# Separate places for ScalarE's and VectorE's look-up steps, from two tables over the work list

## The reference

```python
def _ghost_linear(x, idx, lut):
    w = lut[idx]                                  # weights are looked up: idx is 0..15
    return jnp.einsum('bsh,oh->bso', x, w)

# attention, on the layer-normed x (2, 2048, 512):
q, k, v = x @ Wq, x @ Wk, x @ Wv
attn_scores = jnp.einsum('bes,bfs->bef', qT, kT) / np.sqrt(16)   # 512 x 512 for each batch
attn_weights = softmax(attn_scores); out = (attn_weights @ vT).T @ Wo

# ffn, on the layer-normed x: INTER = 1376, HIDDEN = 512
h = silu(_ghost_linear(x, gate_idx, lut)) * _ghost_linear(x, up_idx, lut)
return _ghost_linear(h, down_idx, lut)

x = x + attn(layernorm(x));  x = x + ffn(layernorm(x))
```

## Time and profile before

| | before |
|---|---|
| median of 3 runs | 1107.08 us (1107.05 to 1108.62) |
| the profiled execution | 1108.86 us, span 1107.0 us |
| busy over the span | PE 1028.1 us (93%), PEld 844.5 (76%), DVE 491.6 (44%), ACT 467.8 (42%), POOL 137.8 (12%) |
| mean granted TensorE clock | 0.973 of full speed |

### The profile page before, as it was taken

The page is one execution under the profiler, slowest core; times in us unless marked ns, Lnnn a source line. Parts: engine busy times, 40 slices in busy tenths (PEclk is TensorE's granted clock), DMA queues, the critical chain, the costliest instruction groups (busy, mean ns, idle before and its releaser), DMA issues.

```text
span 1107.0 us, 13011 instructions
## 1 busy us (share of the span) xinstructions
PE 1028.1 (93%) x4744; PEld 844.5 (76%) x4744; DVE 491.6 (44%) x1016; ACT 467.8 (42%) x753; POOL 137.8 (12%) x135
## 2 busy tenths in 40 slices
PE   5888986979889897999999999999999999999997
PEld 4777775767668775788888888888888888888885
DVE  5786867978878987332213122312221222212001
ACT  4987767777867884122122212211221222122110
POOL 4422000000000000002011111111111111111111
PEclk9988998989979999999999999999999999999999
DMA  8853010230101114530022000201020010000000
GB/s 280 266 198 91 8 60 6 84 119 6 46 8 65 60 51 158 207 129 1 1 76 77 1 1 1 78 1 62 15 76 1 1 41 36 1 1 38 1 1 38
DMA packets 31756, 66.04 MB, mean 60 GB/s; under 512 B 3584, under 2 KB 17168, under 8 KB 27088
## 3 DMA queue, kind: packets, MB, share of 16 engines
q1 hardware_dynamic: 26912, 63.06, 15.9%
q10 hardware_dynamic: 4752, 2.16, 0.7%
q0 software_dynamic: 32, 0.01, 0.1%
HBM read 44.18 MB, written 21.04 MB: 59 GB/s over the span
## 4 chain that ended last, share of the span: by engine, by line
PE 66%; DVE 12%; ACT 12%; issue 8%; POOL 1%; DMA 1%; ACTq 0%; POOLq 0%; DVEq 0%
PE bank L1050 34%; PE bank L1058 19%; PE bank L992 8%; ACT part L791 4%; DVE part L1237 3%; PE bank L1093 2%; DVE picked L1237 2%; ACT picked L791 1%; PE bank L1006 1%; PE bank L1039 1%; DVE bn L1214 1%; DVE w_lo L1253 1%; ACT idx_out L872 1%; DVE part L1275 1%; ACT xg_n L882 1%
## 5 line engine op out<-in xcount | busy, mean ns | idle before, releaser
L1050 PE MATMUL bank<-x2t_hi,w_hi 128*128 128x512 f32 (+1 forms) x704 | 278.3, 395 | 22.6 <-ACT h_gate L944 10.3
L1050 PE MATMUL bank<-x2t_hi,w_lo 128*128 128x512 f32 (+1 forms) x704 | 276.8, 393 | 0.0
L1050 PE MATMUL bank<-x2t_lo,w_hi 128*128 128x512 f32 (+1 forms) x704 | 276.6, 393 | 0.0
L1450 DVE TENSOR_TENSOR h_full<-bank,h_gate 128x512 f32<-128x512 f32 (+1 forms) x66 | 45.6, 691 | 396.6 <-PE bank L1050 396.6
L1050 PEld LDWEIGHTS bank<-x2t_hi,w_hi 128*128 128x128 f32 (+1 forms) x704 | 132.1, 188 | 55.6 <-issue 20.6
L791 ACT ACTIVATE part<-high_bit,lut,lut_step 128x512 f32<-128x512 uint8 x198 | 155.4, 809 | 27.3 <-DVE part L1237 24.9
L1050 PEld LDWEIGHTS bank<-x2t_lo,w_hi 128*128 128x128 f32 (+1 forms) x704 | 132.1, 188 | 30.3
L1050 PEld LDWEIGHTS bank<-x2t_hi,w_lo 128*128 128x128 f32 (+1 forms) x704 | 132.4, 188 | 29.5
L740 POOL TENSOR_TENSOR h_lo<-h_full,h_hi 128x512 fp32r<-128x512 f32 (+1 forms) x66 | 85.2, 1291 | 508.1 <-ACT h_hi L968 508.1
L965 ACT ACTIVATE h_gate<-bank 128x512 f32<-128x512 f32 (+1 forms) x66 | 39.4, 598 | 256.3 <-PE bank L1050 256.3
L1058 PE MATMUL bank<-w_hi,h_hi 128*128 128x512 f32 (+1 forms) x324 | 129.6, 400 | 0.1
(11 more groups left out here) (148 smaller groups left out, 1353.3 us busy)
## 6 DMA issues: line engine op xcount, KB each, us to landing
xg<-in_L_attn_x SPq DMA_DIRECT2D x8, 1024.0 KB, 6.3
out_dram<-x1a SPq DMA_DIRECT2D x5, 1024.0 KB, 3.9
x1a<-in_L_attn_x SPq DMA_DIRECT2D x4, 1024.0 KB, 4.8
x1b<-in_L_attn_x SPq DMA_DIRECT2D x3, 1024.0 KB, 4.8
m_hi<-m_scratch SPq DMA_DIRECT2D x3, 1024.0 KB, 5.1
m_lo<-m_scratch SPq DMA_DIRECT2D x3, 1024.0 KB, 7.2
out_dram<-x1b SPq DMA_DIRECT2D x3, 1024.0 KB, 3.9
idx_raw<-in_L_ffn_gate_idx SPq DMA_DIRECT2D x10, 256.0 KB, 6.2
```

Of the source, the lines that this page charges most:

```text
L1050: last = pe.matmul(tile[0:n, :], a, x, start=(k == 0 and j == 0), stop=(k == K - 1 and j == 2))
L1450: dve.tensor_tensor(h_full[0:n, :], bank[5][0:n, :], h_gate[0:n, :], ALU.mult).then_inc(h_done, 1)
```

## The change

The entries `look` and `built` leave the list, and with them `OPS`, `share`, `room` and the leaf tables. Each engine's look-up becomes a generator of single instructions (ScalarE: a leaf, a fetch, a copy to `w_hi`, 294 steps; VectorE: a find, a merge, a leaf, a `w_lo`, 429 steps). Two strings, `ACT_LOOKS` and `DVE_LOOKS`, have one digit (base 36) for each entry of the list: how many steps that engine takes ahead of that entry. The order of the look-up instructions among themselves is the same on both engines, and so are the other entries and their order, the waits, tiles and banks. Only which other instruction each step stands in front of is different, and no longer the same for both engines.

```diff
-        LEAVES_NEXT = {4: [1], 5: [0], 6: [3], 7: [2], 8: [5]}
-        LEAVES_SAME = {1: [6], 2: [7]}
...
-        def normalised(n, limit):
-            timeline.append(("norm", n))
-            look(1 if n < K * (number[(SCORE, 0)] + 1) else 2, limit)
-            timeline.append(("norm_low", n))
...
+        def normalised(n):
+            timeline.extend([("norm", n), ("norm_low", n)])
...
-            look(1, room(n))
             timeline.append(("take_low", n))
...
-        def share(cost):
-
-            passed[0] += cost
-            look(early + late * min(passed[0], whole) // whole - looked[0] if passed[0] < whole else OPS * U - looked[0], U)
...
+        ACT_LOOKS = (
+            "0000000000000000000000000000000000000000000000000000000000000000000000000000000000000001000000000000"
+            "1000000000101000000000000000000000030000000000000000000000000000000004000300000000000000000000000000"
+            "0000000300000000000000000000000000000000300000000000000000300000000010020200000000000500301020040030"
+            "0400300300500020000020000040000020000200002000040002000000000000000000000000000000600030000300400300"
+            "0030030000200500002002000200005000000010103000000003040000300000600205000020000007000100030500000000"
+            "020000060400060400304001050005050010500204000504003040020500040600106001080003050020400103"
+        )
+        DVE_LOOKS = (
+            "0000000000000000000000000000000000000000000000000000000000000000000000000000000000000000020000000001"
+            "0000000000000000000000010000000300000000000000000400000000000000000005000000030000000000000000000000"
+            "0000200000000000000200000000000000000010000000000003000000300000030000100000070000000030070005006004"
+            "0040050040026000030000040000060000030000300000006000040300000000000000000000000000070003000040060030"
+            "00045000000430000006200000420003000070011000600000003010200100900000a0200000008030006010007010000000"
+            "00200000d02000d020070200702000d010060100803000c010080200604000d020050400902000c050040300b"
+        )
+
+        def with_looks(counts, steps):
+            for k, entry in enumerate(timeline):
+                for _ in range(int(counts[k], 36) if k < len(counts) else 0):
+                    next(steps)
+                yield entry
...
+            def look_up():
+
+                yield from make_leaves(0, LEAVES[:LEAVES_AHEAD])
+                for u in range(U):
+                    yield from make_leaves(u, LEAVES[LEAVES_AHEAD:])
+                    if u + 1 < U:
+                        yield from make_leaves(u + 1, LEAVES[:LEAVES_AHEAD])
+                    act.wait_ge(picked_done, u + 1)
+                    if u + 3 < U:
+                        fetch_idx(u + 3)
+                        yield
+                    weight_high(u)
+                    yield
...
-            for stage, arg in timeline:
+            for stage, arg in with_looks(ACT_LOOKS, look_up()):
```

More of the change, by code:

```diff
@@ L280, in tile_of @@
             return picked[u % 2] if j == 0 else part[{1: one, 2: 1, 3: 2, 4: 3, 5: five, 6: one, 7: 2}[j]]
[L282 to L289, removed]
         def make_leaf(eng, u, j):
@@ L305, in preln_attention_ghost_ffn @@
         timeline = []
[L306 to L313, removed]
         def settle(g):
@@ L430, in preln_attention_ghost_ffn, with prepare @@
         second_plan = ("E10 E0 T0 E1 A0 T1 E2 A1 T2 E3 A2 T3 E4 A3 E5 E6 E7 X0 X1 E8 X2 X3 E9").split()
[L431 to L435, removed]
-        pair_order, second_down_order = [], []
-        passed = [0]
-        def share(cost):
-            passed[0] += cost
-            look(early + late * min(passed[0], whole) // whole - looked[0] if passed[0] < whole else OPS * U - looked[0], U)
-        def prepare(b, kind, i, looks):
+        pair_order, second_down_order = [], []
+        def prepare(b, kind, i):
             if kind == "T":
-                timeline.append(("turn", (b, i)))
-                looks()
-                timeline.extend([("turn_high", (b, i)), ("turn_low", (b, i))])
+                timeline.extend([("turn", (b, i)), ("turn_high", (b, i)), ("turn_low", (b, i))])
             elif kind == "A":
-                timeline.append(("attend", (b, i)))
-                looks()
-                timeline.append(("add", (b, i)))
+                timeline.extend([("attend", (b, i)), ("add", (b, i))])
                 if i == T - 1:
@@ L455, in prepare @@
             elif kind == "X":
-                timeline.append(("x2", (b, i)))
-                looks()
-                timeline.extend([("x2_high", (b, i)), ("x2_low", (b, i))])
+                timeline.extend([("x2", (b, i)), ("x2_high", (b, i)), ("x2_low", (b, i))])
         for step in first_plan:
             kind, i = step[0], int(step[1:])
-            cost = free_ns[kind]
             if kind in "GH":
@@ L465, in preln_attention_ghost_ffn @@
                 pair_order.append(item)
-                timeline.append(("gate_up", item))
-                share(cost // 2)
-                timeline.append(("silu", item))
+                timeline += [("gate_up", item), ("silu", item)]
                 if len(pair_order) == 1:
                     timeline.append(("ln1", 1))
-                share(cost - cost // 2)
                 timeline += [("h_full", item), ("h_high", item), ("h_low", item)]
@@ L474, in preln_attention_ghost_ffn @@
                 timeline.append(("down", (0, i)))
-                share(cost)
             else:
-                prepare(1, kind, i, lambda: share(cost))
-        assert looked[0] == OPS * U
+                prepare(1, kind, i)
         timeline += [("y", 0), ("stats1", 2), ("ln1", 2)]
@@ L784, in fetch_idx, with make_leaves @@
                 act.dma_start(idx_in[u % 3][:], idx_dram[u]).then_inc(idx_back[u % 3], 16)
-            def make_leaves(k):
-                if k == 0:
+            def make_leaves(u, some):
+                if u == 0:
                     act.wait_ge(step_made, 1)
-                for u, j in leaves_at(k):
+                for j in some:
                     tile, high, step, entry = make_leaf(act, u, j)
                     act.activation(tile, high, ACT.Identity, bias=entry, scale=step).then_inc(leaf_made, 1)
+                    yield
             def weight_high(u):
                 c, kind = u // 3, u % 3
-                act.wait_ge(picked_done, u + 1)
-                if u + 3 < U:
-                    fetch_idx(u + 3)
                 if u == 12:
@@ L922, in _ @@
                     act.copy(lo[:, 1, 0:P], turned[2][:, P:2 * P]).then_inc(mirror_taken, 1)
-                if stage == "look":
-                    make_leaves(arg)
-                if stage == "built":
-                    weight_high(arg)
                 if stage == "first":
@@ L1355, in _ @@
             first = one_block[0]
-            looks = look_up()
-            for stage, arg in timeline:
+            for stage, arg in with_looks(DVE_LOOKS, look_up()):
                 if stage == "lut_step":
@@ L1408, in _ @@
                                              op0=ALU.mult, op1=ALU.subtract).then_inc(product_lo, 1)
-                if stage == "look":
-                    next(looks)
                 if stage == "first":
```

42 lines of the change are left out of this document (18 added, 24 removed).

## The result

| | before | after |
|---|---|---|
| median (4 runs each) | 1107.85 us (1107.05 to 1108.86) | 1052.50 us (1051.26 to 1053.55) |
| ratio, 95% interval | | 0.950 (0.9483 to 0.9516) |
| profiled execution; its span | 1108.86; 1107.0 | 1051.26; 1049.5 |
| mean granted TensorE clock | 0.973 | 0.997 |

The change is worth 5%, 55 us. Sign and mechanism were right, and so was the place behind 108 us. About 22 us of gain were missed, and half of them lie in one stretch, the gram, for which I had put down nothing.

The account below looks back on a forecast made before the run. From 108 to 429 us PE and VectorE have equal work and lose 58.5 us waiting for each other. Terms -7.2 - 3.0 - 4.2 - 5.4 - 10.6 - 7.6 = -38, less 3 given back: -35, 1072 us; range 1061 to 1091.

Parts of the forecast that it names:

- the gram's term: Gram, up to 108 us: ScalarE is the full engine, so 0 gain, with bounds of -3 and +3 us.
- PROD and SCORE: Stages ahead of MIX 0: added look-up steps hide in the chain's waits, cost 0, upper bound +11.2 us.
- MIX 0 to FOLD 0: From MIX 0 to FOLD 0: PE waits 1.8 instead of 9.1 us, -7.2; clock behind it holds, -3.0.
- FOLD 0 to the first gate: Stretch behind FOLD 0's start: 3 of the 6.2 us wait stay, -3.2, and less slow clock, -1.
- G0 to G3 with the transposes' wait: Pairs G0 to G3, up to the second x2 transposes: -5.4 for the pairs; 11.3 us in all by stretch.
- x2: The x2 transposes' two waits up to G5: -7.1 us and clock -3.5; 2.9 us from second transposes to G5.
- G5 to G10: Last look-up stretch: idle and slow clock go, but new waits on `w_lo` come at G9 and G10: -7.6 us.
- The 3 us given back: Whole kernel: 3 us taken off the summed gain for hand-overs between engines priced at nothing, -38 to -35.
- (a): Rival: only the early half comes, to x2, -20 us, 1087, since VectorE and PE are balanced later; chance 0.18.
- (b): Rival: PE's gate waits on the single `h_gate` stay, +9 us, 1081; chance 0.08.
- (c): Rival: nearly all of it comes (friction none, gram -3, deadline waits hidden), -45 us, 1062; chance 0.14.
- (d): Rival: slower, VectorE is the bound and SCORE's added steps don't hide, +3.4 us, 1110.5; chance 0.08 with a cancelled sum.

Follow-up runs that it names:

- n166: Changed code with new places only up to entry 166 (early gram), the places of the kernel before from there on: 1106.47 us, ratio 0.999 to before.
- v1: Changed kernel with the last look-up steps of tiles 28 and 31 moved ahead of h_low (1, 7) and h_full (1, 9): 1047.92 us, again 1048.18.
- n488: Changed code with new places up to entry 488 (G3's end), the places of the kernel before from there on: 1066.33 us, ratio 0.9642 to before.

## Why the prediction was right or wrong

**The failed step is the gram's term**, "ScalarE is the full engine there ... I take 0, bounds -3". It gave 10.4 us in the traces and 1.1% (12 us) alone. Over 33 to 108 us of the trace before, ScalarE was busy for 62.14 us of 75, and VectorE for 55.19:

```profile
33.00:108.00 75.00, 61.88 (x391) 55.14 (x391) 55.19 (x124) 62.14 (x108) 21.75 (x25) 0.91 0.56 179
```

I had the clock's dips there in view, but cut my windows from 108 us on and called the engine full without reading its busy time ahead of that. It was nearly full up to 60 us (25.81 of 27) and idle for a quarter from there. What was lost there is the same coupled waiting that I had found behind 108 us. PE's gaps from 33 us to the first product fall from 13.4 to 9.6 us, and its 13.7 us at half clock to none: 3.8 + 13.7 / 2 = 10.7, near the 10.4 of the table (an estimate: it counts PE busy in all of the half clock). About two thirds of it is clock, which I had priced there nowhere. In the second trace of the changed kernel the gaps are 8.0 us and 3.4 us of half clock are left, 5.4 + 10.3 / 2 = 10.6 against 9.6 measured, so about half is clock there. The new places of the first half of the stage, where ScalarE is indeed nearly full, gave nothing alone (n166).

**PROD and SCORE** (0; 3.2 measured). That the added steps hide in the chain's waits was right. The items of the chain, from `norm_low` to `norm_low`, take 3.80 to 4.00 us in the first half (4.28 before) and 3.17 to 3.79 in the second, much as I had worked them out:

```profile
134.25 0.72 DVE L1376 SCALAR_TENSOR_TENSOR mat_x_lo<-full,srec,mat_x_hi 128x512 fp32r<-128x512 f32 x1
138.25 0.73 DVE L1376 SCALAR_TENSOR_TENSOR mat_x_lo<-full,srec,mat_x_hi 128x512 fp32r<-128x512 f32 x1
142.05 0.73 DVE L1376 SCALAR_TENSOR_TENSOR mat_x_lo<-full,srec,mat_x_hi 128x512 fp32r<-128x512 f32 x1
145.22 0.75 DVE L1376 SCALAR_TENSOR_TENSOR mat_x_lo<-full,srec,mat_x_hi 128x512 fp32r<-128x512 f32 x1 [0.38 <-ACT mat_x_hi L885]
148.66 0.76 DVE L1376 SCALAR_TENSOR_TENSOR mat_x_lo<-full,srec,mat_x_hi 128x512 fp32r<-128x512 f32 x1
152.45 0.75 DVE L1376 SCALAR_TENSOR_TENSOR mat_x_lo<-full,srec,mat_x_hi 128x512 fp32r<-128x512 f32 x1
```

That they leave PE's start of MIX 0 where it was, wasn't right: PE's waits of 0.92 and 2.54 us before it became 1.20 in all.

**MIX 0 to FOLD 0** (7.2; 7.0): right, with the wait 1.83 as forecast at 1.8. The clock behind it holds (3.0; the next stretch).

**FOLD 0 to the first gate** (6.2 with the clock; 9.9). I kept 3 us of the 6.2 wait and it is 1.22, and the clock behind the gate is whole. **G0 to G3 with the transposes' wait** (11.3; 14.0): of the 2.7 over, 1.7 is the rest of that gate's clock (5.4 us at half, I took 1 of 2.7). **x2** (2.9; 2.9): the wait's floor was worked out as 1.4 and is 1.65. **G5 to G10** (10.4; 10.5): right, and the two new waits on `w_lo` were named with 1.3 and 3.5 us and are 1.37 and 2.56. v1 shows that 1.7 us of these 3.9 were places; of the rest no run tells. (In the second trace this stretch takes 117.4 us, so 12.0 us less than before: the match of 10.5 is partly luck with the half clock.)

**The 3 us given back** for hand-overs weren't: VectorE's waits for leaves are 3.6 us over 277, and the stages' gains add up. So the 22.8 us between 57.8 and the forecast's 35 are 10.4 + 3.2 + 3.7 + 2.7 + 3, less 0.2 at MIX 0.

**The rivals.** (a), only the early half, is false: the late stretches came as forecast, and n488 against all shows 1.4% from them. (b), the waits on `h_gate` stay, is false: 10.3 us became none with the single `h_gate` in place. The Trainium skill (Perfetto Trace Analysis, Optimization Strategy) names too few buffers as a possible reason for a repeated gap; here the gap went with the buffer count unchanged, so it was the order ahead of the instruction that PE waited for. (c), nearly all of it, was nearest and still 9.5 us short, since its -3 for the gram was my bound. (d) is false by its own point, items of 5.5 us: they take 3.2 to 4.0. MIX 0 comes 13.5 us earlier, 10.4 of them from the gram. The budget from which all of them were cut (58.5 us over 108 to 429) was too small because it began at 108 us; of it 57.8 - 10.4 = 47 us came. (In the earlier trace rows, counted from 1, PE is full from slice 17 on and not from 16, which ends at 443 us; no term hangs on it.)

## What to carry to other kernels

Where filler work is woven into two in-order engines, ask at each place which engine is waiting there and for whom, and give each its own list: the partner's steps belong elsewhere (tying ScalarE's to VectorE's places lost 36 of the 50 thousandths gained). Read busy time by stretch over all the stages that a change touches, and split a stage in two before calling an engine full in it. Where PE's short waits disappear, count the half-clock stretches behind them too: in the gram they were a half to two thirds of the gain.

## What the runs showed of the hardware

- The clock's dips differ between executions of one kernel. The two traces of the changed kernel have one stretch at 0.50 behind 33 us (367.5 to 370.9, behind the 2.56 us wait) and two (56.8 to 60.2 and 162.6 to 166.1, and none behind the same 2.56 us wait); the mean clock is 0.997 and 0.995. With PE full, such a stretch costs 3.4 / 2 = 1.7 us: scatter that no edit explains, and the reason why a difference of 1 us in one pair of traces isn't read here.
- In the gram of before, VectorE's merge took 1.10 us instead of 0.74 while GpSimd's casts were running, and the subtraction behind it 1.08 instead of 0.69. Up to 440 us the two traces list 370 merges one by one. 15 of them overlap a cast of GpSimd, and 6 of these take 1.00 to 1.15 us; none of the other 355 takes over 0.9. So the long ones all go with a cast, but not every cast lengthens a merge; what decides it is open.

```profile
74.84 3.29 POOL L759 CAST idx_bf<-idx_raw 128x512 bf16<-128x512 int32 x4
```
```profile
76.59 1.10 DVE L1237 COPY_PREDICATED part<-bit_mask,part 128x512 f32<-128x512 uint8 x1
77.58 1.08 DVE L1253 TENSOR_TENSOR xg_lo<-xg_n,xg_hi 128x512 fp32r<-128x512 f32 x1
```
